# The chunk recurrence's state product in two column halves, with a block diagonal state

## What is computed

```python
x = x + (weights(adj) @ (layernorm(x) @ W + B))      # weights: exp(-2 (1/adj - 1)^2) where adj < 1, else 0
x = x + mamba2(layernorm(x)) @ W_lin + b_lin         # chunked recurrence, 8 heads of 64, state 64
x = x + mamba1(layernorm(relu(adj @ layernorm(x) @ gcn_w + gcn_b)))
x = x + experts(layernorm(x))                        # 2 of 8 experts
```

```python
Y_off = exp(A_cum) * (C @ h)                         # what the state before the chunk gives
h     = exp(A_cum[-1]) * h + B.T @ (decay * x * dt)  # the state after it
```

## Time and profile before

| | us |
|---|---|
| median of 3 runs | 2362.43 |
| lowest and highest | 2361.44, 2364.4 |
| span of the profiled execution | 2360.5 |
| TensorE busy | 2203.0 |
| VectorE busy | 1799.9 |
| ScalarE busy | 1567.2 |
| GpSimd busy | 1146.1 |

### The profile page before, as it was taken

The page is one execution under the profiler, slowest core; times in us unless marked ns, Lnnn a source line. Parts: engine busy times, 40 slices in busy tenths (PEclk is TensorE's granted clock), DMA queues, the critical chain, the costliest instruction groups (busy, mean ns, idle before and its releaser), DMA issues.

```text
span 2360.5 us, 26229 instructions
## 1 busy us (share of the span) xinstructions
PE 2203.0 (93%) x8900; PEld 1388.7 (59%) x8900; DVE 1799.9 (76%) x2083; ACT 1567.2 (66%) x2541; POOL 1146.1 (49%) x926
## 2 busy tenths in 40 slices
PE   7998999999999999989999999999999987787998
PEld 4544545555555556546766666776766663444886
DVE  5666767777777765324989898999989898996665
ACT  5677686778686845425676867677676868774444
POOL 2101322222231313203988888888988888890000
PEclk9999999999999999999999999999999999798999
DMA  6243332333232323233423232333333221312121
GB/s 234 71 138 100 106 116 90 125 99 123 82 125 91 116 88 134 90 100 108 132 92 125 90 123 84 122 102 103 117 103 119 90 88 43 119 36 98 36 81 45
DMA packets 117111, 241.22 MB, mean 102 GB/s; under 512 B 8258, under 2 KB 65986, under 8 KB 116594
## 3 DMA queue, kind: packets, MB, share of 16 engines
q1 hardware_dynamic: 107906, 207.14, 26.8%
q0 software_dynamic: 8528, 31.36, 4.0%
q10 hardware_dynamic: 544, 1.05, 0.1%
HBM read 219.20 MB, written 20.32 MB: 101 GB/s over the span
## 4 chain that ended last, share of the span: by engine, by line
PE 65%; POOL 11%; ACT 10%; DVE 9%; issue 5%; DMA 0%; ACTq 0%; DVEq 0%; POOLq 0%
PE ps L684 13%; PE ps L726 10%; POOL dB L2301 7%; PE ps L970 5%; POOL acc L2283 2%; PE ps L848 2%; PE ps L822 2%; DVE h L1472 2%; PE ps L954 2%; PE ps L708 2%; ACT ps L1658 2%; ACT L1656 1%; POOL du L2297 1%; PE ps L754 1%; PE ps L752 1%
## 5 line engine op out<-in xcount | busy, mean ns | idle before, releaser
L1472 DVE TENSOR_TENSOR_SCAN h<-ps,hst,dB 128x512 f32<-128x512 f32 x512 | 637.2, 1271 | 64.5 <-ACT ps L1658 57.7
L2301 POOL TENSOR_TENSOR dB<-du,bc 128x512 f32<-128x512 f32 x512 | 648.9, 1290 | 61.2 <-DVE h L1472 58.4
L684 PE MATMUL ps<-wgt,msg 128*128 128x512 f32 x1024 | 488.4, 597 | 2.1 <-DVE xb L1180 2.1
L1658 ACT ACTIVATE ps<-dt,cols 128x512 f32<-128x512 f32 x512 | 351.0, 690 | 177.0 <-DVE h L1472 174.8
L726 PE MATMUL ps<-raw,msg 128*128 128x256 f32 x1792 | 443.1, 384 | 0.9 <-ACT hb L1658 0.9
L970 PEld LDWEIGHTS ps<-consts,h 128*128 128x128 f32 x2048 | 250.4, 144 | 221.2 <-issue 73.5
L970 PE MATMUL ps<-consts,h 128*128 128x128 f32 x2048 | 322.1, 283 | 61.0 <-DVE acc L1434 29.8
L726 PEld LDWEIGHTS ps<-raw,msg 128*128 128x128 f32 x1792 | 328.3, 193 | 76.2 <-issue 42.4
L684 PEld LDWEIGHTS ps<-wgt,msg 128*128 128x128 f32 x1024 | 189.6, 192 | 205.6 <-issue 203.9
L1658 ACT ACTIVATE wgt<-wgt 128x1024 f32<-128x1024 f32 x256 | 257.9, 1047 | 50.2 <-DVE wgt L1145 48.8
L2283 POOL TENSOR_TENSOR acc<-acc,part 128x512 f32<-128x512 f32 x174 | 226.2, 1300 | 61.3 <-ACT part L1658 60.2
(11 more groups left out here) (318 smaller groups left out, 3574.0 us busy)
## 6 DMA issues: line engine op xcount, KB each, us to landing
raw<-in_adjT SPq DMA_DIRECT2D x256, 512.0 KB, 3.6
bc<-tmp_bc SPq DMA_DIRECT2D x64, 512.0 KB, 4.7
E<-tmp_bc POOLq DMA_DIRECT2D x32, 512.0 KB, 4.2
xb<-in_xT POOLq DMA_DIRECT2D x8, 512.0 KB, 4.3
tmp_x<-xb POOLq DMA_DIRECT2D x8, 512.0 KB, 4.2
x<-tmp_x SPq DMA_DIRECT2D x8, 512.0 KB, 5.2
tmp_x<-x SPq DMA_DIRECT2D x8, 512.0 KB, 4.8
msg<-in_W SPq DMA_DIRECT2D x4, 1024.0 KB, 10.7
```

What stands on the lines that cost most here:

```text
L684: x = e.matmul(P[d][:, :], msg[:, j, d * 128:(d + 1) * 128], wgt[g % NW][:, l, :], start=j == 0, stop=j == NJ - 1)
L1472: e.tensor_tensor_scan(hr[n % 3][:, m, :], PS[4 + k % 2].t[:, :], dBr[k % 4][:, :], hst[:, n % 16, m:m + 1], ALU.mult, ALU.add).then_inc(S ...
L1658: return e.activation(out, in_, func, bias=bias, scale=scale)
L2301: e.tensor_tensor(dBr[k % 4][:, :], du[:, m, :], bcr[i % 3][:, n % 2, :], ALU.mult).then_inc(S("dB"), 1)
```

## The change

The state is kept block diagonal: heads 0 to 3 (columns 0 to 255) on partitions 0 to 63, heads 4 to 7 (columns 256 to 511) on partitions 64 to 127, zeros elsewhere. The state product becomes two, each of 64 columns of weights and 256 moving columns, with their outputs on the lower and the upper half of the partitions of the same bank. C has to stand on both halves of the partitions, so the convolution's last tile goes to tile 5, and three silus follow, each waiting for the one before: B to tile 4's lower half, C to tile 5's lower half, C in place in the upper half. The zeros are now in tile 4's upper half. Waits on the count of silus change from 6 to 7 a block, and from 4 to 5 for TensorE.

```diff
+        def half_state(a, g, c=0):
+            return a[64 * g:64 * g + 64, c:c + 256].rearrange("p (h q) -> p h q", h=4)
...
-        hd = sb(cA, "hd", [64, 512])
+        hd = sb(cA, "hd", [128, 512])
...
-                    w.wait_ge(S("sil"), 6 * ib + 4)
+                    w.wait_ge(S("sil"), 7 * ib + 5)
...
-                    e.matmul(St.ps[:, :], bn[:, :], xdec[:, :], start=True, stop=True).then_inc(St.full, 1)
+                    for g in range(2):
+                        i = e.matmul(St.ps[64 * g:64 * g + 64, 0:256], bn[:, 0:64], xdec[:, 256 * g:256 * g + 256],
+                                     start=True, stop=True)
+                    i.then_inc(St.full, 1)
...
-                    c, at = cc[:, m, :], 20 * ib + 4 * m
+                    c, at = cc[:, m + m // 4, :], 20 * ib + 4 * m
...
-                    e.tensor_tensor(h0[0:64, :], hd[:, :], St.ps[0:64, :], ALU.add).then_inc(St.evac, 1)
+                    for g in range(2):
+                        i = e.tensor_tensor(half_state(h0, g, 256 * g), half_state(hd, g, 256 * g), half_state(St.ps, g), ALU.add)
+                    i.then_inc(St.evac, 1)
...
-                    w.wait_ge(S("sil"), 6 * ib + 6)
+                    w.wait_ge(S("sil"), 7 * ib + 7)
...
-                for i in range(2):
-                    act(cc[0:64, 4 + i, :], cc[64 * i:64 * i + 64, 4, :], ACT.Silu).then_inc(S("sil"), 1)
+                act(cc[0:64, 4, :], cc[0:64, 5, :], ACT.Silu).then_inc(S("sil"), 1)
+                w.wait_ge(S("sil"), 7 * ib + 3)
+                act(cc[0:64, 5, :], cc[64:128, 5, :], ACT.Silu).then_inc(S("sil"), 1)
+                w.wait_ge(S("sil"), 7 * ib + 4)
+                act(cc[64:128, 5, :], cc[64:128, 5, :], ACT.Silu).then_inc(S("sil"), 1)
...
-            e.memset(ccs[1][64:128, 5, :], 0.0).then_inc(S("zero"), 1)
+            e.memset(ccs[1][64:128, 4, :], 0.0).then_inc(S("zero"), 1)
...
-                    e.tensor_tensor(heads(hd[:, :]), heads(h0[0:64, :]), ecd[0:64, 2, s, :, None].broadcast_to([64, 8, 64]),
+                    e.tensor_tensor(heads(hd[:, :]), heads(h0[:, :]), ecd[:, 2, s, :, None].broadcast_to([128, 8, 64]),
```

More of the change, by code:

```diff
@@ L2254, in _ @@
             w.wait_ge(S("zero"), 2)
-            e.memset(ccs[0][64:128, 5, :], 0.0).then_inc(S("zero"), 1)
+            e.memset(ccs[0][64:128, 4, :], 0.0).then_inc(S("zero"), 1)
             for b in (NB - 2, NB - 1):
```

## The result

| | us |
|---|---|
| median after (8 runs, 2364.06 to 2374.05) | 2369.22 |
| median before, beside it (8 runs) | 2362.05 |
| ratio | 1.0029, interval 1.002 to 1.0038 |
| span of the profiled execution after (before: 2360.5) | 2372.2 |
| forecast | 2370.6 (2363.5 to 2379) |

The changed kernel is slower by about 7 us. (Two executions further down, 4210.43 of the halves alone and 3809.37 of the GpSimd copy, had a mean granted clock of 0.81 and 0.55; the ratios leave them out.) The forecast of +8.2 was close, but two of its terms were wrong and a third was missing, and they nearly cancelled. The working was right for the silus only.

A forecast was written before the change was run, and what follows sets the result against it. TensorE, busy 117.75 of 120 us in the steady part, was taken as the bound. State product 3.0, silus 5.0 and h0 sum 0.2 make 8.2 us; 2362.4 + 8.2 = 2370.6 us, range 2363.5 to 2379.

The forecast's parts named there:

- TensorE, 32 chunks: State product: 0.31 us for changing array width minus 0.215 us overlap, +0.10 us a chunk, 3.0 us for 32.
- silus, 8 blocks: ScalarE's third silu at each block's last convolution tile: +0.66 us in all eight blocks, 5.3 us, 5.0 after block 0's clock.
- sum for h0, block 7: VectorE's L1270 split into two 64x256 sums: hidden in blocks 0 to 6, exposed in block 7, 2 x 0.1 = 0.2 us.
- low granted clock: Clock taken as full through the steady part; only block 0's low level was considered, so no added loss elsewhere.
- The failing step: State product's four passes: issued in order, only passes 2 and 3 overlap, giving three lengths, 0.645 us, a gain of 0.215.
- Rival 2: State product: both passes of the halves overlap, -3.8 + 5.2 = +1.4 us, 2363.8 us; chance 0.10.
- the switch: Going into and out of fewer array columns around the state product, with unhidden weight loads: 0.31 us a chunk.
- Rival 4: State product: going over to halves is free; -8.6 us, 2353.8 us with both passes overlapped, -1.7 with middle overlap; chance 0.08.
- Rival 1: State product: the halves run one behind another, 9.9 + 5.2 = 15.1 us, 2377.5 us; chance 0.29.
- Rival 3: Third silu absorbed by a hole in ScalarE's run, leaving TensorE's 3.0 and 0.4, 2365.8 us; chance 0.08.
- At nothing: GpSimd's hd on 128 partitions, moved zeroing, unchanged L806 and L790 shapes, and silu-count waits cost nothing; hd at most 0.4 us.
- The test named in the prediction: State product: third pass starting within nanoseconds of the second would show overlap; 0.215 us behind it, serial halves.

The follow-up runs named there:

- halves alone: Kernel before with only the state product in two column halves and the h0 sum in two of 64x256; 2363.06 us, ratio 1.0.
- GpSimd copy: Changed kernel with the third silu replaced by a GpSimd copy of C to the upper half; 2365.66 us, ratio 1.001.
- four quarters issued half by half: Kernel with state product and h0 sum in two halves, each half's product now two matmuls of 128 moving columns, first half's both issued first; 2359.77 us, one run.
- product whole in one half: Kernel before with the state product as one matmul of 64 weight columns and all 512 moving columns, nothing beside it; 2372.83 us, one run.
- spare in the slack: Kernel before with one more 64x512 ScalarE instruction a block, beside the second chunk, into an unread tile; 2362.68 us, ratio 0.9999.
- one silu: Kernel before with two 64x512 silus made one of 128x512, VectorE moving C to tile 5, state product whole; 2360.57 us, ratio 0.9989.
- product in one half: Kernel before with the state product as two matmuls of 64 weight and 256 moving columns, both on partitions 0 to 63; 2373.61 us, one run.
- both orders of the quarters: State product as four matmuls of 128 moving columns, h0 sum in two: half by half 2359.77 us, alternating halves 2361.72 us, one run each.
- one silu with halves: Kernel with state product and h0 sum in two halves, plus one 128x512 silu for two and VectorE moving C; 2359.39 us, ratio 0.9987.
- silus alone: Changed kernel with the whole state product, h0 sum and hd of before, keeping the B and C tiles and third silu; 2370.27 us, ratio 1.0033.
- silus and a spare one in the run: Kernel with the third silu but the whole state product, plus a 64x768 ScalarE silu right behind the third; 2380.76 us, ratio 1.0082.

## Why the forecast was right in its number and wrong in its working

| term | forecast | measured | |
|---|---|---|---|
| TensorE, 32 chunks | +3.0 | -2.5 (32 x -0.079) | wrong sign |
| silus, 8 blocks | +5.0 | +5.3 | right |
| sum for h0, block 7 | +0.2 | +0.6 in the wait of L806, halves alone | too small |
| low granted clock | 0 | +3.3 in the profiled execution | missing |
| sum, or median | +8.2 | +7.2 | |

**The failing step** is the one on the state product, in the prediction's words: "the two passes of the first half use the same half of the array, and the first pass of the second half is issued behind them: only pass 2 and pass 3 belong to different halves and stand next to each other". The passes overlap in both pairs, a gain of 0.42 us and not 0.215; four quarters issued half by half overlap too. Rival 2 had this mechanism, at a chance of 0.10, and its term of -3.8 missed the -2.5 by the size of the switch, 0.34 where it took 0.31. I chose the middle between two bounds for a reason from instruction order, which no row carried.

**The switch** was sized from L770 and L924 at 0.31, inside 0.28 to 0.35; alone it measured 0.34. The Trainium skill, TensorEngine Tiling (Array Packing), section Key Properties, says that changing the mode drains TensorE and that tiles work in parallel; the traces agree with both, with 0.34 us lost and 0.42 us won. Both belong in one sum: for this product of 512 columns in f32, full overlap is worth 0.08 us after the switch. Rival 4, a free switch, is refuted by the product whole in one half (+0.34 a chunk). Rival 1 is refuted by the same rows as the forecast.

**The silus** went as worked out: a loop without slack, 0.66 us a block in every block, 0.74 us of wait at L747. Rival 3 (absorbed) is refuted: the group has 24 members, and the wait grew from 0.09 to 0.74. Against it the prediction said that L744 waits seven times; these are seven weight loads, and the waits that matter are those of the blocks 1 to 5. An instruction of the same length in the slack cost nothing, and more of it in the run cost nearly its full length.

**The sum for h0** was bounded by L1138, whose 256-column sums overlap in a row. The two new sums don't: they take 0.42 us each, 0.85 us together, the upper end of my 0.66 to 0.84, and delay L806 by 0.18 us where I took 0.1. (They differ from L1138 in being on 64 partitions, and on different ones; which of it matters was not tried.) The other 0.4 us of the 0.6 is TensorE's gain, which block 7 doesn't pass on; the prediction named such a loss, up to 0.5 us, but didn't put it in the sum.

**The missing term.** The prediction named the clock only in block 0. It didn't ask what a wait of 0.74 us at a place where TensorE stood still for 0.09 us does to the clock afterwards. In the traces of this case, low stretches between 230 and 960 us come as follows:

| kernel | wait at the block boundary | low stretches |
|---|---|---|
| before, halves alone, GpSimd copy, spare in the slack, one silu | 0.07 to 0.11, or none | 0 |
| product whole, product in one half, both orders of the quarters | 0.07 to 0.09 | 0 |
| one silu with halves | 0.69 in block 0 only | 1, at 236.0 |
| silus alone | 0.75 | 1 |
| changed kernel | 0.74 | 2 |
| silus and a spare one in the run | 0.75, and 0.52 at L788 | 4 |

Each of these stretches begins 1.6 to 3.0 us after the product that had a wait of 0.7 us starts, and the kernels without such waits have none in this part. There are 17 such waits in the four executions, and 8 stretches. The length of a wait alone doesn't explain it: the kernel before stands still longer ten times in this part, twice in each of five blocks, for instance

```profile
428.22 1.12 PE L633 MATMUL ps<-tmp,consts 128*128 128x512 f32 x2 [1.14 <-DVE tmp L1302]
...
439.82 3.72 PE L860 MATMUL ps<-W,z 128*128 128x256 f32 x16 [1.03 <-DVE z L1311]
```

and no low stretch follows. So the link is one by place and number. That the wait at L747 is the cause was not tested by itself, and why only some of these waits are followed by a stretch stays open. It was not tried how many low stretches an average run of the changed kernel has: the profile is one execution. With one stretch the measured terms sum to -2.5 + 5.3 + 0.6 + 1.65 = 5.0, with the two of the profile to 6.7, and with the stretch that moved in block 7 to 8.4, beside a median of +7.2 (about +4.7 to +9 by the interval). That the forecast came within 1 us of it is luck: it had TensorE's term 5.5 us too high, and nothing for the clock.

**At nothing** was right: `hd` on 128 partitions (the GpSimd copy has it, with the block of the halves alone), the moved zeros, and the counts of the waits.

The test named in the prediction did its work: "the third pass of L811's successor starting within some nanoseconds of the second" was meant to show the overlap, and the trace shows more than that. The passes start in two pairs.

## What to carry to other kernels

Packing a product of 64 columns into both halves of the array brought its four passes from 1.00 to 0.58 us, but going to the narrower mode and back had a price (0.34 us here), so it pays only where the passes saved take longer than that, or where several such products stand together. The packing's gain was smaller than what its data layout cost ScalarE. When a layout needs one instruction more, look for an engine or a moment with slack before counting its size: the same 0.6 us cost 5 us behind the silus and nothing beside the second chunk. And where a change adds a wait to the engine that sets the pace, look at its granted clock behind it, and at where the low stretches of both kernels fall: one in front of a wait cost nothing, the same one behind it 1.7 us.

## What the runs showed of the hardware

- Passes in the two column halves of TensorE start 0.007 to 0.013 us apart, and not in the order of the program: a second half that stands behind four passes of the first starts with it. On one half, passes of 256 columns start 0.22 to 0.27 us apart.
- Going to products of 64 columns and back costs 0.34 us: 0.09 going in, 0.05 between the passes, 0.2 coming out.
- VectorE: two neighbouring sums of 64x256 whose products lie on different partitions take 0.42 us each, 0.85 together, with no overlap; one of 64x512 takes 0.60 to 0.68.
- Behind 8 of 17 waits of 0.7 us at the dt product, TensorE's granted clock was 0.50 for 3.4 us, at 1.6 to 1.7 us each; behind waits of 1.02 to 1.14 us at two other products it stayed full.
- A low stretch of 3.4 us cost 1.7 us where TensorE went on without a wait, and nothing where a wait of 2.04 us stood behind it (block 7).
